# End of the gram stage: the last column multiplied behind the last blocks, its operands read in another order, filler matmuls ahead of them, and the closing matmuls interleaved

## The reference, cut to what matters

```python
B, C, H, W = feature.shape            # G = 16 groups, Cg = 8 channels, K = 3
Hm, Wm = (H - K + 1, W - K + 1)       # 126 x 94
slices = [feature[:, :, ki:ki + Hm, kj:kj + Wm] for ki in range(K) for kj in range(K)]
patches = jnp.stack(slices, axis=2)
motif = patches.reshape(B, G, Cg * 9, L).reshape(B, G, 9, Cg, L)
gram = jnp.einsum('bgjcl,bgjdl->bgjcd', motif, motif)
sq = jnp.einsum('bgjcl,bgjcl->bgjc', motif, motif)
d2 = sq[..., :, None] + sq[..., None, :] - 2.0 * gram
nn_idx = jnp.argmin(jnp.where(eye, jnp.inf, d2), axis=-1)
u_max = jnp.max(nn_idx, axis=-1)
c_max = jnp.sum(nn_idx == u_max[..., None], axis=-1)
motif_nn = jnp.take_along_axis(motif, u_max[..., None, None], axis=3)
term = jnp.floor(motif * motif_nn * c_max[..., None, None] / Cg)
```

## Time and profile before

| What | Value |
|---|---|
| Median of 3 runs | 1486.88 us (1481.56 to 1488.61) |
| Own time of the profiled execution | 1487.57 us |
| Its span (first to last instruction) | 1485.6 us |
| Mean granted clock of TensorE | 0.958 of 2.4 GHz |
| PE busy | 1316.8 us (89%) |
| PEld busy | 1054.3 us (71%) |
| DVE busy | 1136.3 us (76%) |
| ACT busy | 887.3 us (60%) |

### The profile page before, as it was taken

One profiled execution on the slowest core, in us unless ns is written; L12 is line 12 of the kernel. 1 busy time (PEld: TensorE's weight loads), 2 busy tenths in 40 slices (PEclk: granted clock), 3 DMA queues, 4 the chain that ended last, 5 costly groups with the idle time before them and its releaser, 6 DMA issues. The chain is left out here.

```text
span 1485.6 us, 34009 instructions
## 1 busy us (share of the span) xinstructions
PE 1316.8 (89%) x13586; PEld 1054.3 (71%) x13586; DVE 1136.3 (76%) x1896; ACT 887.3 (60%) x1013; POOL 656.0 (44%) x672
## 2 busy tenths in 40 slices
PE   3899998986999499999969999989959968999998
PEld 1888897985999255555539899879949954555554
DVE  6587777468773699999945677755887838999998
ACT  3566653212552499999935555531135508999996
POOL 4888893332320253352037898814413113344400
PEclk9999999998999699999979999999979978999999
DMA  5466631693133445464255766309405225274533
GB/s 210 128 200 194 197 106 43 205 279 130 44 125 133 171 132 123 125 168 106 74 185 181 222 204 186 88 17 281 118 1 214 108 89 181 77 190 105 148 71 102
DMA packets 75875, 210.26 MB, mean 142 GB/s; under 512 B 15306, under 2 KB 15414, under 8 KB 72774
## 3 DMA queue, kind: packets, MB, share of 16 engines
q1 hardware_dynamic: 61214, 158.10, 34.0%
q0 software_dynamic: 6720, 36.93, 9.3%
q10 hardware_dynamic: 7784, 13.07, 3.2%
HBM read 91.54 MB, written 67.04 MB: 107 GB/s over the span
## 5 line engine op out<-in xcount | busy, mean ns | idle before, releaser
L1761 PE MATMUL acc<-rnd,ident 128*128 128x376 f32 x1152 | 394.5, 486 | 16.2 <-ACT rnd L1738 16.2
L1761 PEld LDWEIGHTS acc<-rnd,ident 128*128 128x128 f32 x1152 | 217.5, 193 | 138.1 <-ACT rnd L1738 17.6
L955 PE MATMUL ps_a<-wa,xa 128*128 128x192 f16 x1536 | 298.1, 247 | 10.6 <-DMA xc<-low 8.5
L955 PE MATMUL ps_a<-wb,xb 128*128 128x192 f16 x1536 | 296.9, 247 | 0.0
L1586 DVE TENSOR_TENSOR prod<-fc,near 128x1504 f32<-128x1504 f32 x144 | 247.3, 1717 | 28.6 <-DMA near<-near 19.1
L1733 ACT ACTIVATE rnd_m<-prod,plus_round,scale 128x1504 f32<-128x1504 f32 x144 | 235.8, 1637 | 45.6 <-DVE prod L1586 35.1
L573 POOL TENSOR_TENSOR vt<-z 96x256 f32<-96x256 f32 x248 | 256.0, 1052 | 9.1 <-ACT z L849 7.4
L1697 DVE SCALAR_TENSOR_TENSOR over<-prod,scale,rnd 128x1504 bf16<-128x1504 f32 x144 | 255.5, 1777 | 0.0
L1641 POOL DMA_INDIRECT near<-f_planes,index x56 | 156.8, 2800 | 216.0 <-DVE prod L1586 208.2
L1738 ACT ACTIVATE rnd<-rnd_m,minus_round 128x1504 f32<-128x1504 f32 x144 | 223.2, 1550 | 4.7
L955 PEld LDWEIGHTS ps_a<-wa,xa 128*128 128x128 f16 x1536 | 151.2, 98 | 14.3 <-DMA xc<-low 9.8
(11 more groups left out here) (331 smaller groups left out, 2367.9 us busy)
## 6 DMA issues: line engine op xcount, KB each, us to landing
xb<-xa ACTq DMA_DIRECT2D x64, 195.0 KB, 2.7
f_planes<-img SPq DMA_DIRECT2D x8, 1536.0 KB, 14.1
fc<-f_planes SPq DMA_DIRECT2D x16, 768.0 KB, 5.4
v_a<-xa SPq DMA_DIRECT2D x40, 260.0 KB, 2.6
v_b<-xb SPq DMA_DIRECT2D x40, 260.0 KB, 3.1
xa<-v_a SPq DMA_DIRECT2D x40, 260.0 KB, 4.8
xb<-v_b SPq DMA_DIRECT2D x40, 260.0 KB, 5.3
near<-near SPq DMA_DIRECT2D x96, 107.9 KB, 2.3
```

The lines of the kernel that those rows point to most:

```text
L955: mm = lambda a, w, first, end: nc.tensor.matmul(out(i), a, w, start=first, stop=end)
L1761: nc.tensor.matmul(o(m), k["ident"][:, :], rnd[:, n % RNDS, BR * m:BR * m + BR, :], start=False, stop=False, skip_group_check=True)
```

## The change

It has four parts. `last_column()` moves from ahead of the last two blocks to behind them. Its matmuls read the moving side in the order in which it lies, (j i p), and write the output with the steps that this needs: neighbouring columns now go to places 9 floats apart. Eight matmuls of 480 columns of zeros are put behind the last transposes. And the joins and folds become functions of a third and are issued as join 0, join 1, fold 0, join 2, fold 1, fold 2, with the counts that ScalarE (`JOINED`) and VectorE (`FOLDED`) wait for set to that order.

```diff
         NORM_EVERY = 6 if b == 0 else 3
         SUM_FIRST = UNITS - 2 * (H // SUM_ROWS) + 1
         PER = 6
+        JOINED, FOLDED = (1, 2, 4), (3, 5, 6)
         sums = lambda: ps_s[:, 0:2 * GN].rearrange("p (a g) -> p a g", g=GN)
         piece = lambda j: img[:, :, PIECE * j:PIECE * j + PIECE]
         half = lambda j, h: split[j % 2][:, h, 0:W, :]
                                      ).then_inc(gram_out2 if j == 2 else gram_out, 1)
             for j in range(3):
                 n = min(PER, MG - PER * j)
-                act.wait_ge(post_pe, j + 1)
+                act.wait_ge(post_pe, JOINED[j])
                 nc.scalar.activation(g_turn[:, PER * j:PER * j + n, :],
                                      ps_t[j][0:MR, 0:n * MR].rearrange("p (g r) -> p g r", r=MR),
                                      ACT.Copy).then_inc(post_act, 1)
                     a = (g * COLS + WM - 1 - (C - CHUNK)) * CK
                     out = ps_t[g // PER][0:MR, (g % PER) * MR:(g % PER) * MR + MR]
                     for t in (turned_hi[1], turned_lo[1]):
-                        nc.tensor.matmul(out.rearrange("r (p i j) -> r p i j", i=3, j=3), t[0:HM, a:a + MR],
-                                         turned_hi[1][0:HM, a:a + MR].rearrange("x (j i p) -> x p i j", i=3, j=3),
+                        nc.tensor.matmul(out.rearrange("r (p i j) -> r j i p", i=3, j=3), t[0:HM, a:a + MR],
+                                         turned_hi[1][0:HM, a:a + MR].rearrange("x (j i p) -> x j i p", i=3, j=3),
                                          start=False, stop=False, skip_group_check=True)
 
             m = 0
                 while m < BLOCKS and first_need(m) <= u - LAG:
                     gram(m)
                     m += 1
-            last_column()
+            for _ in range(8):
+                nc.tensor.matmul(acc[3][:, 0:4 * CW], k["zeros"][:, 0:P], k["zeros"][:, 0:4 * CW], start=False,
+                                 stop=False, skip_group_check=True)
             for side in range(2):
                 for m_ in range(m, BLOCKS):
                     gram(m_, range(8 * side, 8 * side + 8))
-
...
+            last_column()
+
+            def joined(third):
+
+                for g in range(PER * third, min(PER * third + PER, MG)):
+                    if g in (0, 8):
+                        pe.wait_ge(gram_out if g == 0 else gram_out2, 2)
+                    for j in range(3):
+                        last = nc.tensor.matmul(ps_t[third][0:MR, (g % PER) * MR:(g % PER) * MR + MR],
+                                                g_half[:, g, CK * j:CK * j + MR], k["order3"][:, j, :],
+                                                start=False, stop=(j == 2), skip_group_check=True)
+                last.then_inc(post_pe, 1)
+
             order = k["order3"][0:MR, 0, :]
...
+            def folded(third):
+                pe.wait_ge(post_act, third + 1)
+                for g in range(PER * third, min(PER * third + PER, MG)):
+                    out = ps_t[third][0:MR, (g % PER) * MR:(g % PER) * MR + MR]
+                    nc.tensor.matmul(out, g_turn[:, g, :], order, start=True, stop=False)
+                    last = nc.tensor.matmul(out, order, g_turn[:, g, :], start=False, stop=True)
+                last.then_inc(post_pe, 1)
+
+            joined(0)
+            joined(1)
+            folded(0)
+            joined(2)
+            folded(1)
+            folded(2)
             nc.tensor.matmul(ps_a[0][0:MR, 0:MG * MC], k["ident"][0:MR, 0:MR],
                              k["own_big"][:].rearrange("p g d -> p (g d)"), start=True, stop=False)
             pe.wait_ge(pick_pe, 1)
             for j in range(3):
                 n = min(PER, MG - PER * j)
                 third = slice(PER * j, PER * j + n)
-                dve.wait_ge(post_pe, 3 + j + 1)
+                dve.wait_ge(post_pe, FOLDED[j])
                 c.then_wait(nc.vector.tensor_tensor(
                     g_all[:, third, :], ps_t[j][0:MR, 0:n * MR].rearrange("p (g r) -> p g r", r=MR),
                     k["same_block"][:, :].unsqueeze(1).to_broadcast([MR, n, MR]), ALU.mult))
```

More of the change, by code:

```diff
@@ L1318, in _ @@
                     gram(m_, range(8 * side, 8 * side + 8))
[L1320 to L1328, removed]
@@ L1329, in _ @@
-            order = k["order3"][0:MR, 0, :]
[L1330 to L1337, removed]
+            last_column()
```

## The result

Over 20 runs each, the changed kernel takes 1480.04 us (median; 1476.39 to 1488.75) and the kernel before 1488.11 us (1479.88 to 1499.66). The ratio is 0.995 with a 95% interval of 0.9931 to 0.9968, so the change saves 7.4 us, between 4.8 and 10.3. The profiled execution after took 1478.87 us with a span of 1477.0 us.

The account below looks back on a forecast made before the run. Bound: the serial TensorE chain from last transposes to joins. 1.63 + 3.36 + 0.55 + 2.08 = 7.62 us against 10.19 and 10.57 saves 5.5 us: from median 1486.88 to 1481.4 us, range 1476.5 to 1488.0.

Parts of the forecast that it names:

- The sum: TensorE from last transposes to joins: 7.62 us, gaining 2.57 us in image 0 and 2.95 in image 1, together 5.5.
- Zeros: Behind the last transposes: eight matmuls cost 1.63 us, cover a 0.93 us wait, and 0.70 us stick out as whole cost.
- Clock: In the last two blocks: full clock for all 64 matmuls, 3.36 us against 4.51 us in image 0.
- The last column: Behind the blocks: clearing stays 0.55 us, 32 matmuls at 65 ns instead of 131 take 2.08 us.
- this shape is the nearest: Last column's spacing: taken from fp32 folds with 72 stationary and 72 moving columns, 65 ns each.
- Rival (b): Last column: stepped output makes PSUM the slow side at 131 ns; 1485.6 us, or 1489.1 with clock falling; chance 0.18.
- My estimate of 60 ns for 72 columns: Last column's stationary load at columns over 1.2 ns: column 1.92 us, gain 0.3 us larger over both images.
- Folds: Folding thirds as they come gains VectorE slack, no time; first join to last third stays 11.05 us, within 0.1.
- (a): Last column runs at its columns' pace, 31.5 ns spacing; 7.7 us gained in all, 1479.2 us; chance 0.13.
- (c): Last column's stepped output is read and written, 262 ns spacing; loss 7.1 us, 1494.0 us; chance 0.05.
- (d): Zeros do not hold the clock, which falls during side 0 of the blocks; 2.9 us gained, 1484.0 us; chance 0.05.
- (e): Something else ends the gram stage, so nothing changes; 1486.9 us; chance 0.03.

Follow-up runs that it names:

- new read alone: Kernel before, with only the last column's matmul reading its moving side as it lies and writing in steps; 1475.84 us, ratio to before 0.9896.
- old read: Changed kernel, with the last column, still behind the blocks, reading in steps and writing contiguously as before; 1488.76 us, ratio to before 1.0014.
- zeros alone: Kernel before, with only the eight matmuls of zeros added behind the last transposes, ahead of the last column; one run, 1483.75 us.
- the run with the plain output: Changed kernel with its 72 stationary columns, the last column's output written as it comes, the reordering left out; one run, 1476.3 us.

## Why the prediction was right, point by point

*The sum.* 5.5 us forecast, 5.70 us on the path (7.62 us against 7.53), 7.4 us (4.8 to 10.3) in the whole time. The time of 1480.04 us lies 1.4 us under the forecast of 1481.4, which went from the median of three runs; 20 runs put the kernel before 1.2 us higher than those. That it lies so close is in part luck: the medians differ by 8.1 us, 2.6 us more than the sum, and the higher start hides about half of that. The path does not show these 2.6 us, and the interval of the gain holds the sum with and without them.

*Zeros.* Costed at 1.63 us of which 0.93 us cover a wait; 459.46 to 461.11 is 1.65. But "0.70 us stick out ... that is their whole cost" failed: the step compared the zeros with the wait as it was ahead of the last column. With the blocks next in line, block 29 fills the wait itself, and the zeros cost 1.56 us in each image. I saw that block 29 needs one unit less, and did not carry it into the price.

*Clock.* Full clock for all 64 matmuls of the blocks, as forecast. I named the wait and the slow matmuls together as what went ahead of the fall. The runs separate them: the wait without slow matmuls (new read alone) left the clock at 1.00 in both images; the slow column without a wait brought it down in one image of two, twice (old read, zeros alone). Over all profiled runs the clock fell at the column in 4 of 6 passages with the stepped read and in none of 16 with the read as it lies. So the slow matmuls were the part that mattered, and the wait had no part that a run shows. That the zeros are not needed was not in the forecast.

*The last column.* 65 ns forecast, 62 measured, but for a wrong reason: that the numbers agree is luck. The step "this shape is the nearest" took the stationary side of fp32 rows as what sets the spacing. The runs put the output's steps in its place: 35 ns becomes 62 with 72 stationary columns, 32 becomes 61 with 128. My argument against rival (b), that a doubled price of writing would stay hidden, had the size right and its place wrong: writing is what is seen. Rival (b) named the mechanism, and only its price (131 ns) was off. The Trainium skill's rule (PSUM — Partial Sum Buffer, Specifications) that patterns that are not contiguous slow matmuls holds here, with a factor of 1.8 to 1.9; the change still gains, since the read's steps cost more, 131 ns. My estimate of 60 ns for 72 columns, from the Trainium skill (TensorE: Matmul & The Clock Gate, LDWEIGHTS), does not hold as a bound on the spacing of fp16 matmuls: the run with the plain output had 35 ns, and the measurement decides.

*Folds.* Costed at nothing, 11.05 us expected and 11.07 measured; with the old order 11.08. Fold 1 ends at the same time in both orders, and VectorE's gain of 1.54 us on third 0 becomes 1.55 us of idle time. The joins did not wait for `g_half`, as forecast: they begin at 466.99, right behind the last column.

*Rivals.* (a) did not come: columns' pace needs the plain output. (c) and (d) did not come, and (e) is excluded by the gain.

## What to carry to other kernels

Take a change apart before keeping it whole: here the order in which one matmul reads and writes brought 7.1 us on the path over both images, the move another 1.7, the filler gave back 3.1, and the reordered folds did nothing. Filler matmuls are to be priced against the wait that is left after the reordering, since work that needs less than the last input may already fill it. And where a permutation can sit on a matmul's read or on its output, measure both: here 131 ns against 62, and 32 to 35 with neither (which leaves the permutation out, and so serves to measure only).

## What the runs showed that was not expected

Part of the kernel's scatter of several microseconds arises far ahead of the change, in a stretch of the attention stage that is the same in all programs. Busy time by stretch of the changed kernel, and under it of the run with 128 stationary columns:

```profile
250.00:270.00 20.00, 16.23 (x141) 1.00 0.00 1
270.00:300.00 30.00, 28.83 (x665) 1.00 0.93 279
```

```profile
250.00:270.00 20.00, 16.71 (x101) 0.82 0.00 1
270.00:300.00 30.00, 30.00 (x553) 0.84 0.63 181
```

In the second the granted clock is at 1.2 GHz for part of these 50 us, fewer matmuls get through (553 against 665 in the 30 us), and the gram stage begins at 372.4 instead of 361.8 us. That is over 10 us, more than the whole change brings. In the attention stage of image 1 the same run has a low clock again (0.77 on average between 1000 and 1030 us, where the changed kernel has 1.00) and loses another 7.6 us between the joins of image 0 and the last transposes of image 1. Its path from the transposes to the joins is 7.53 us in both images, that of the changed kernel, so its 1496.35 us says nothing on its edit. Why the clock falls there in one run and not in another stays open.

Second, the stepped read costs the same 131 ns at 1.2 and at 2.4 GHz: in the kernel before, the matmuls of the column behind the fall at 466 us start as far apart as those ahead of it. Third, the same column brought the clock down in one image and not in the other of one execution; what decides between the two stayed open and was not tried.
